# The four value products of a unit together, ahead of the next unit's first maximum, in the first attention of a two-layer network

## The reference

```
c_q = x @ Wq_down
c_kv = x @ Wkv_down
q_c = (c_q @ Wq_up).reshape(b, s, N_HEADS, HEAD_DIM)
q_r = (x @ Wq_rope).reshape(b, s, N_HEADS, ROPE)
k_c = (c_kv @ Wk_up).reshape(b, s, N_HEADS, HEAD_DIM)
v_c = (c_kv @ Wv_up).reshape(b, s, N_HEADS, HEAD_DIM)
k_r = x @ Wk_rope
scores = (einsum('bqhd,bkhd->bhqk', q_c, k_c) + einsum('bqhd,bkd->bhqk', q_r, k_r)) / scale
attn = softmax(scores)
out = einsum('bhqk,bkhd->bqhd', attn, v_c).reshape(b, s, N_HEADS * HEAD_DIM)
return out @ Wo
```

## Time and profile before

| | |
|---|---|
| median of 3 runs | 2729.01 us (2726.97 to 2730.4) |
| span of the profiled execution | 2727.7 us |
| the first attention's units 1 to 62 | from 101 to 1500 us of the span |
| TensorE (PE) busy | 2571.7 us, 94% of the span |
| VectorE (DVE) busy | 1579.8 us, 58% |
| ScalarE (ACT) busy | 1129.2 us, 41% |
| GpSimd (POOL) busy | 439.7 us, 16% |

### The profile page before, as it was taken

The page is one execution under the profiler, slowest core; times in us unless marked ns, Lnnn a source line. Parts: engine busy times, 40 slices in busy tenths (PEclk is TensorE's granted clock), DMA queues, the critical chain, the costliest instruction groups (busy, mean ns, idle before and its releaser), DMA issues. The chain is left out here.

```text
span 2727.7 us, 38579 instructions
## 1 busy us (share of the span) xinstructions
PE 2571.7 (94%) x12487; PEld 1838.7 (67%) x12487; DVE 1579.8 (58%) x2919; ACT 1129.2 (41%) x1832; POOL 439.7 (16%) x519
## 2 busy tenths in 40 slices
PE   6999999999999999999999759989999999999996
PEld 3666666666666666666666436658778778778774
DVE  5666666666666666666666260137566566566566
ACT  3455555555555555555555230014234234243231
POOL 0101010101010101010100010004343343242320
PEclk8899999999999999999999969989999999999998
DMA  5122121212121212121211240010110110110001
GB/s 190 44 43 49 41 49 41 49 41 49 41 49 41 49 41 49 41 49 41 49 41 41 69 138 0 0 54 24 39 38 0 38 38 0 38 38 0 16 1 51
DMA packets 46693, 116.86 MB, mean 43 GB/s; under 512 B 5313, under 2 KB 22721, under 8 KB 40514
## 3 DMA queue, kind: packets, MB, share of 16 engines
q1 hardware_dynamic: 46658, 116.40, 16.3%
HBM read 71.81 MB, written 10.49 MB: 30 GB/s over the span
## 5 line engine op out<-in xcount | busy, mean ns | idle before, releaser
L407 DVE TENSOR_REDUCE row_max<-ps_max 128x1 f32<-128x512 f32 x1024 | 678.1, 689 | 294.0 <-PE ps_max L472 270.4
L361 ACT ACTIVATE probs<-ps_score 128x1024 f32<-128x1024 f32 x512 | 525.6, 1027 | 123.8 <-PE ps_score L487 92.5
L472 PE MATMUL ps_max<-KX,Q 68*128 68x512 f32 x1024 | 396.3, 418 | 46.0 <-DMA KX<-content_k 41.2
L485 PE MATMUL ps_score<-Q,K 128*128 128x512 f32 x1024 | 409.1, 400 | 0.5 <-ACT probs L361 0.5
L487 PE MATMUL ps_score<-Q,K 97*128 97x512 f32 x1024 | 405.7, 396 | 0.0
L472 PEld LDWEIGHTS ps_max<-KX,Q 68*128 68x128 f32 x1024 | 194.3, 190 | 207.1 <-issue 150.3
L401 DVE TENSOR_TENSOR Q<-ps_x,Q 64x512 fp32r<-64x512 f32 x256 | 176.5, 690 | 240.7 <-ACT Q L356 238.9
L356 ACT ACTIVATE Q<-ps_x 64x512 fp32r<-64x512 f32 x256 | 151.9, 593 | 365.3 <-PE ps_x L457 363.8
L497 PE MATMUL ps_o<-probs,V_slot 128*32 128x512 f32 x2048 | 245.8, 598 | 1.1 <-ACT probs L361 1.1
L485 PEld LDWEIGHTS ps_score<-Q,K 128*128 128x128 f32 x1024 | 194.2, 190 | 54.9 <-ACT probs L361 12.1
L487 PEld LDWEIGHTS ps_score<-Q,K 97*128 97x128 f32 x1024 | 194.8, 190 | 41.0
(11 more groups left out here) (217 smaller groups left out, 3952.8 us busy)
## 6 DMA issues: line engine op xcount, KB each, us to landing
Q<-Q SPq DMA_DIRECT2D x64, 512.0 KB, 4.3
w_raw<-in_w_qrope SPq DMA_DIRECT2D x32, 512.0 KB, 3.7
wq_raw<-in_wq SPq DMA_DIRECT2D x8, 1024.0 KB, 5.6
wo_raw<-in_wo SPq DMA_DIRECT2D x8, 1024.0 KB, 4.9
w_raw<-in_w SPq DMA_DIRECT2D x6, 704.0 KB, 4.1
Q<-content_q SPq DMA_DIRECT2D x64, 64.0 KB
K<-content_k SPq DMA_DIRECT2D x64, 64.0 KB
wkv_raw<-in_wkv SPq DMA_DIRECT2D x8, 512.0 KB, 3.5
```

What stands on the lines that cost most here:

```text
L361: act.activation(probs[:, j, 2 * half:2 * half + 2, :], ps_score[half][:, :, :], ACT.Exp, scale=SCALE).then_inc(exped, 1)
L407: dve.tensor_reduce(row_max[:, t, j:j + 1], ps_max[t % 2][:, :], axis=AXX, op=ALU.max)\
L472: pe.matmul(ps_max[t % 2][:, :], Q2[0:KC0, b, j, t * P:(t + 1) * P], KX[0:KC0, b, j, :], start=True, stop=True).then_inc(max_made, 1)
L485: pe.matmul(ps_score[half][:, k, :], K1[:, b, t * P:(t + 1) * P], Q1[:, b, j, :], start=True, stop=False)
```

## The change

Two entries of `ORDER` change places with one: `v20 v30` come to stand ahead of `m00` in place of behind it. Nothing else is changed; the same instructions run with the same operands and the same waits.

```
         ORDER = [(step[0], int(step[1]), int(step[2])) for step in (
-            "v00 v10 m00 v20 v30 m01 q00 m02 q10 m03 m10 q20 m11 s00 l00 m12 s01 m13 "
+            "v00 v10 v20 v30 m00 m01 q00 m02 q10 m03 m10 q20 m11 s00 l00 m12 s01 m13 "
             "s10 o00 m20 s11 m21 s20 m22 m23 s21 m30 s30 m31 m32 s31 m33").split()]
```

## The result

| | before | after |
|---|---|---|
| median | 2727.99 us (4 runs, 2726.18 to 2730.4) | 2662.07 us (4 runs, 2660.67 to 2665.5) |
| ratio | | 0.9759 (95% interval 0.9746 to 0.9773) |
| span of the profiled execution | 2727.7 us | 2658.9 us |

The change saves 65.9 us by the medians, 2.4%. The forecast was a median of 2664 us, within 2657 to 2678 us; its sum had said 64.8 us.

A forecast was written before the change was run, and what follows sets the result against it. TensorE's in-order stream, busy 97% in units 1 to 62, was taken as the bound. Content wait 45.6 us plus passage 19 us gave 64.8 us off 2727.7, a 2662.9 us span; forecast median 2664 us, range 2657 to 2678.

The forecast's parts named there:

- its sum: From v00 to m02, 6.125 us before and 5.08 after: 1.045 us a unit, 62 units, 64.8 us saved.
- The content wait: TensorE idling at m00 behind a content load; hidden by v20 v30, saving 0.735 us a unit, 45.6 us.
- The third rival: Content wait ahead of m00 is moved, not hidden; only 19 us saved, about 2710 us; chance 0.04.
- The passage: One passage from 32-column value products to full-width ones and back no longer made; 0.31 us a unit, 19 us.
- The block of four: Four value steps standing together, v00 to m00, taken as 3.57 us from unit 63's row.
- The second rival: Small wait at m02 behind VectorE, or m00 behind a late sequencer or full queue; 2676 us; chance 0.12.
- m02 behind VectorE: m02's weight load, at 1.28 us, meets VectorE's release at 1.27; cost taken as nothing, 12 us kept for the range.
- Slower, by VectorE or by the clock: Fifth rival: VectorE's takings end a unit, 0.985 us longer each, about 2790 us, or TensorE's clock falls; chance 0.03.

The follow-up runs named there:

- the pair without loads: Content loads left out behind the first group: order of the kernel before 2681.43 us (ratio 0.9818), changed order 2660.99 us (0.9742).
- two and three: Three pieces: content loads left out behind the first group, changed kernel's order made v00 v10 m00 v20 m01 v30; 2701.37 us; two pieces, order of before, 2681.43 us.
- the first experiment: Against the changed kernel, m00 put behind the third value step and ahead of the fourth (v00 v10 v20 m00 v30); 2684.72 us, ratio 0.9836.
- The extra reductions: Changed kernel plus an unused VectorE reduction ahead of the taking of m00: 128 columns 2666.55 us (ratio 0.9772), 512 columns 2691.95 us (0.9867).

## Why the prediction was right

**What bounds.** TensorE's stream sets the units' length: of the 66.2 us that the units lost, 65.9 lie between `v00` and `m02`, 1.06 us in the mean, 62 times, and the rest of the unit moved by 0.2 us in all.

**The content wait** (0.735 us a unit, 45.6 us). Shown by the pair without loads: 46.6 us by the medians, 45.5 by the profiles' units. It was hidden and not moved: TensorE idled ahead of none of the 62 `m00`, so no landing came later than the block's end; without the loads the changed kernel gained nothing more; and with three value steps as cover the latest `m00` stood 3.06 us behind `v00`, against 3.00 before. The third rival falls.

**The passage** (0.31 us a unit, 19 us). Shown three times: 20.4 us between one piece and two, 19.9 us between two and three, and 22.7 us between the changed kernel and the first experiment, of which 2.8 us are the content's. The Trainium skill (TensorEngine Tiling (Array Packing), "Tiling Modes") says that changing the tiling mode drains TensorE. The runs agree, with 0.32 to 0.33 us for a pair of changes; they don't tell the drain apart from the change of number format, since the narrow products are also the f32 ones, while the full-width ones around them work on operands that are split into a high and a low part. Why the weight load doesn't run ahead at such a change stays open as well.

**The block of four.** Taken from unit 63, 3.57 us; measured 3.57 in the inner units. The second rival's part that rests on a queue that is full isn't seen: no idling stands between the block and `m00`. The Trainium skill (TensorE: Matmul & The Clock Gate, "Architectural detail: the array is 16× 32×32, not 1× 128×128") gives the queue 64 instructions. No run here shows whether the block fills them: the trace has 32 loads and 32 matmuls for it, the program 16 matmuls.

**m02 behind VectorE.** Taken at nothing with a margin of 0.01 us, and it was nothing: 5.06 to 5.08 us to `m02`, against 5.08, with the load 1.28 us behind `m00`, as worked out. The reason given was partly too kind. I had read that a load late by 0.20 us costs nothing, since its own matmul was on time. The trace of before has the cost already, one matmul further:

```profile
745.13 0.40 PE L487 MATMUL ps_score<-Q,K 97*128 97x512 f32 x1
```

This starts 0.27 us behind the matmul at 744.86, where 0.24 is usual. The extra reductions show it again, 0.08 us behind a load that idled 0.25, and that all but 0.11 to 0.12 us of a later release is paid. Had VectorE's taking been 0.2 us longer, the sum would have been 5 us off; that the two met to 0.01 us was fortune, not design.

**Slower, by VectorE or by the clock.** VectorE's waits for products fell from 260.7 to 194.8 us, by as much as the units lost, so it still has idling to give; and the clock stayed at 1.00 in units 1 to 62. But the clock was nearer than the prediction made it: it falls in 15 of 61 units once TensorE idles 1.7 us behind the transposes L531, and before the change it idled up to 1.1 us, two value steps later in the unit, without that.

The sum was 1 us short of the medians' difference (64.8 against 65.9) and 1.4 us short of the units' (66.2). About 1.1 us of that is the rounding of durations that were read from one unit: `v00` to `m02` is 6.137 us before and 5.074 after in the mean, where the sum has 6.125 and 5.08. The forecast of 2664 us stands 1.9 us above the measured median, of which 1 us is that the fourth run of before brought its median down to 2727.99.

## What to carry to other kernels

Where an in-order engine waits for a transfer in the middle of a block of work that is ready, put the whole block ahead of the wait; read how far the worst landing lies behind the block's start and compare it with the block's full length, not with the mean. Count changes between narrow and full-width products on TensorE as a cost of their own, here 0.32 to 0.33 us a pair, even where no record shows idling. When two producers' steps come closer together, look up whether the consumer's release still comes ahead of the next weight load, and look one matmul further than the one that waited.

## What the runs showed of the hardware that was not expected

Behind idling of 1.64 to 1.69 us that returned in each unit of 23.5 us, with short narrow transposes ahead of it and one product behind it, the granted clock fell from 1.00 in 15 of 61 units and cost 1.69 us in each; behind idling of 2.1 to 3.1 us it fell in 21 of 61 and cost 2.13 us in the mean. With up to 1.1 us of idling two value steps further on in the unit, it stood at 1.00 over 1399 us. How much of that difference is the length of the idling and how much its place was not separated, and why it fell in some units and not in others with idling as long stays open.
